# State-space layer on one Trainium2 core: two decoder products, their additions and the store of each batch put off into the next batch's turn

## What is computed

```
fx = _layernorm(u, ln1_g, ln1_b)
Bu = jnp.einsum('ph,blh->blp', B_bar, fx.astype(B_bar.dtype))
_, xs = jax.lax.associative_scan(binop, (lam_el, Bu), axis=1)
y = 2.0 * jnp.real(jnp.einsum('hp,blp->blh', Cc, xs)) + D * fx
y = jax.nn.gelu(y, approximate=False) + res
fy = _layernorm(y, ln2_g, ln2_b)
z = fy @ W_enc.T
z1, z2 = jnp.split(z, 2, axis=-1)
z = z1 * jax.nn.gelu(z2, approximate=False)
y = z @ W_dec.T + fy
```

## Time and profile before

| | us |
|---|---|
| median of 3 runs | 4407.61 |
| lowest and highest | 4402.94, 4409.49 |
| profiled execution, whole | 4405.0 |
| its span, first to last instruction | 4403.3 |
| of it the turns 0 to 7 of the state-space layer | 784.1 |

### The profile page before, as it was taken

The page is one execution under the profiler, slowest core; times in us unless marked ns, Lnnn a source line. Parts: engine busy times, 40 slices in busy tenths (PEclk is TensorE's granted clock), DMA queues, the critical chain, the costliest instruction groups (busy, mean ns, idle before and its releaser), DMA issues. The chain is left out here.

```text
span 4403.3 us, 53838 instructions
## 1 busy us (share of the span) xinstructions
PE 3966.2 (90%) x17283; PEld 2343.6 (53%) x17283; DVE 3071.4 (70%) x3124; ACT 2265.4 (51%) x3601; POOL 1375.6 (31%) x1108
## 2 busy tenths in 40 slices
PE   6999999999999999749999998455799999999999
PEld 5777777777777677414444443234344444444444
DVE  4757575767676766376777775434888879878878
ACT  2858686767676777533333322222445445544544
POOL 2758575757576767521111100213000000000000
PEclk8999999999999999969999999787899999999999
DMA  4323233333333333110111100647110110110110
GB/s 126 89 76 107 76 104 85 99 90 98 90 94 95 90 98 75 68 57 29 57 43 43 43 29 29 179 136 210 66 43 0 43 43 0 43 43 0 43 43 14
DMA packets 114250, 307.91 MB, mean 70 GB/s; under 512 B 47634, under 2 KB 49250, under 8 KB 104306
## 3 DMA queue, kind: packets, MB, share of 16 engines
q1 hardware_dynamic: 105522, 272.56, 20.1%
q0 software_dynamic: 7504, 24.80, 2.2%
q10 hardware_dynamic: 1008, 7.67, 0.5%
HBM read 203.12 MB, written 101.30 MB: 69 GB/s over the span
## 5 line engine op out<-in xcount | busy, mean ns | idle before, releaser
L417 POOL TENSOR_TENSOR probs_lo<-probs,probs_hi 128x512 fp32r<-128x512 f32 x848 | 1172.0, 1398 | 637.7 <-ACT probs L463 617.8
L530 DVE TENSOR_REDUCE maxima<-m_psum 128x1 fp32r<-128x1024 f32 x512 | 625.3, 1222 | 367.4 <-PE m_psum L706 366.6
L462 ACT ACTIVATE probs_hi<-s_psum 128x512 fp32r<-128x512 f32 x1024 | 614.0, 600 | 382.1 <-PE o_psum L735 220.4
L2376 PE MATMUL psum<-mixes,last_weights 128*128 128x512 f32 x1728 | 751.1, 592 | 0.0
L463 ACT ACTIVATE probs<-s_psum 128x512 f32<-128x512 f32 x1024 | 608.2, 594 | 0.0
L2376 PEld LDWEIGHTS psum<-mixes,last_weights 128*128 128x128 f32 x1728 | 327.5, 190 | 409.8 <-issue 409.8
L719 PE MATMUL s_psum<-q_all,k_hi 128*128 128x512 f32 x1024 | 429.7, 420 | 25.6 <-ACT probs L463 25.4
L735 PE MATMUL o_psum<-probs_lo,v 128*112 128x512 f32 x1024 | 411.9, 402 | 13.4 <-DVE probs_lo L610 6.6
L720 PE MATMUL s_psum<-q_all,k_lo 128*128 128x512 f32 x1024 | 403.6, 394 | 0.0
L730 PE MATMUL o_psum<-probs_hi,v 128*112 128x512 f32 x1024 | 403.3, 394 | 0.0
L2383 PE MATMUL psum<-xp,last_weights 128*128 128x512 f32 x864 | 382.2, 596 | 18.3 <-DVEq L2260 13.3
(11 more groups left out here) (327 smaller groups left out, 6025.4 us busy)
## 6 DMA issues: line engine op xcount, KB each, us to landing
xin<-x SPq DMA_DIRECT2D x17, 1536.0 KB, 6.9
xin<-in_x SPq DMA_DIRECT2D x16, 1536.0 KB, 7.5
k_hi<-k_rows_hi SPq DMA_DIRECT2D x128, 192.0 KB, 3.4
xres<-x SPq DMA_DIRECT2D x16, 1536.0 KB, 7.0
k_rows_hi<-stage_hi SPq DMA_DIRECT2D x48, 256.0 KB, 2.1
k_rows_lo<-stage_lo SPq DMA_DIRECT2D x48, 256.0 KB, 2.3
q_rows_hi<-stage_hi SPq DMA_DIRECT2D x48, 256.0 KB, 2.3
q_rows_lo<-stage_lo SPq DMA_DIRECT2D x48, 256.0 KB, 2.5
```

Source lines behind the costliest of these rows:

```text
L417: pool.tensor_tensor(probs_lo[:, u % RING, :], probs[:, u % RING, :], as_f32(probs_hi[:, u % RING, :]), ALU.subtract).then_inc(pool_low.ne ...
L462: nc.scalar.activation(probs_hi[:, u % RING, :], s_psum[:, u % 2, :], ACT.Exp, scale=SCALE)
L530: nc.vector.tensor_reduce(maxima[:, g % 2, tile:tile + 1], source, AX.X, ALU.max, negate=True).then_inc(rows_max.next(), 1)
L2376: ins = nc.tensor.matmul(bank, conv_w[:, t, down, factor, m * P:(m + 1) * P], mixes[:, factor, t, down:down + S, :].rearrange("p a b -> p ...
```

## The change

- A constant EARLY = 4. In turn i the decoder makes products 0 to 3 of batch i after its encoder; products 4 and 5 are made in turn i + 1, after the last norm sum and ahead of that turn's encoder. The last batch makes all six in its own turn. ORDER, and with it the banks, follows.
- VectorE's outputs is split alike: four additions and bn_stats in turn i; two more, with the moments, in turn i + 1 between the second half of turn_in (and the second norm's scaling) and the first norm's scaling.
- SyncE stores batch i - 1 and reloads xres for batch i in turn i, behind the load of xin.
- GpSimd's and ScalarE's sums and squares of the first norm use a tile of their own, first_sums, instead of hid.

```diff
+        first_sums = sb("first_sums", [P, CT, T])
...
+        EARLY = 4
+
+        def early(i):
+            return EARLY if i + 1 < B else 2 * CT
...
+            if i >= 1:
+                ORDER += [("dec", i - 1, n) for n in range(EARLY, 2 * CT)]
             if i >= 0:
-                ORDER += [("enc", i, n) for n in range(4 * CT)] + [("dec", i, n) for n in range(2 * CT)]
+                ORDER += [("enc", i, n) for n in range(4 * CT)] + [("dec", i, n) for n in range(early(i))]
...
-                if i >= 0:
-                    sp.wait_ge(out_made.sem, out_made.at(2 * CT, i))
-                    sp.dma_start(x_out[i:i + 1].rearrange("a (p t) n -> p (a t n)", t=CT), xres[:, :, :].rearrange("p t n -> p (t n)")).then_inc(stored, 16)
-                    if i + 1 < B:
-                        sp.wait_ge(out_measured.sem, out_measured.at(1, i))
-                        sp.wait_ge(stored, 16 * (i + 1))
...
+                if i >= 1:
+                    store(i - 1)
+                    sp.wait_ge(out_measured.sem, out_measured.at(1, i - 1))
+                    sp.wait_ge(stored, 16 * i)
...
+            store(B - 1)
...
-                        at = hid[:, 0, cols(half)]
+                        at = first_sums[:, 0, cols(half)]
...
-                    squares(norm1, hid, f1[i % 2], centred1, squared1, i + 2)
+                    squares(norm1, first_sums, f1[i % 2], centred1, squared1, i + 2)
...
-            def outputs(i):
-                for n in range(2 * CT + 1):
-                    if n < 2 * CT:
+            def outputs(i, first, end):
+                for n in range(first, end + 1):
+                    if n < end:
...
-                    if n > 0:
+                    if n > first:
...
+                if end < 2 * CT:
+                    return
...
+                if batch(i - 1):
+                    outputs(i - 1, EARLY, 2 * CT)
                 if third:
                     scale(norm1, f1[i % 2], inv_made1, scaled1, i + 2)
...
-                    outputs(i)
+                    outputs(i, 0, early(i))
...
-            def fill_dec(i):
-                for n in range(2 * CT):
+            def fill_dec(i, first, end):
+                for n in range(first, end):
                     m, half = n % CT, n // CT
-                    if m == 0:
+                    if m == 0 or n == first:
...
                 if here:
+                    if i >= 1:
+                        fill_dec(i - 1, EARLY, 2 * CT)
                     fill_enc(i)
-                    fill_dec(i)
+                    fill_dec(i, 0, early(i))
```

More of the change, by code:

```diff
@@ L1123, in _, with store @@
         def _(sp):
+            def store(i):
+                sp.wait_ge(out_made.sem, out_made.at(2 * CT, i))
+                sp.dma_start(x_out[i:i + 1].rearrange("a (p t) n -> p (a t n)", t=CT), xres[:, :, :].rearrange("p t n -> p (t n)")).then_inc(stored, 16)
             for i in range(-3, B):
@@ L1129, in _ @@
                     sp.dma_start(xin[:, :], x_in[i + 3:i + 4].rearrange("a (p t) n -> p (a t n)", t=CT)).then_inc(x_loaded, 16)
-                if i >= 0:
-                    sp.wait_ge(out_made.sem, out_made.at(2 * CT, i))
-                    sp.dma_start(x_out[i:i + 1].rearrange("a (p t) n -> p (a t n)", t=CT), xres[:, :, :].rearrange("p t n -> p (t n)")).then_inc(stored, 16)
-                    if i + 1 < B:
-                        sp.wait_ge(out_measured.sem, out_measured.at(1, i))
-                        sp.wait_ge(stored, 16 * (i + 1))
-                        sp.dma_start(xres[:, :, :].rearrange("p t n -> p (t n)"), x_in[i + 1:i + 2].rearrange("a (p t) n -> p (a t n)", t=CT)).then_inc(res_loaded, 16)
+                if i >= 1:
+                    store(i - 1)
+                    sp.wait_ge(out_measured.sem, out_measured.at(1, i - 1))
+                    sp.wait_ge(stored, 16 * i)
+                    sp.dma_start(xres[:, :, :].rearrange("p t n -> p (t n)"), x_in[i:i + 1].rearrange("a (p t) n -> p (a t n)", t=CT)).then_inc(res_loaded, 16)
+            store(B - 1)
             sp.wait_ge(stored, 16 * B)
@@ L1152, in _ @@
                     for half in range(2):
-                        at = hid[:, 0, cols(half)]
+                        at = first_sums[:, 0, cols(half)]
                         pool.wait_ge(squared1.sem, squared1.at(half + 1, i + 2))
-                        pool.tensor_tensor(at, at, hid[:, 1, cols(half)], ALU.add).then_inc(summed_sq1.next(), 1)
+                        pool.tensor_tensor(at, at, first_sums[:, 1, cols(half)], ALU.add).then_inc(summed_sq1.next(), 1)
                         pool.wait_ge(summed_sq1.sem, summed_sq1.at(2 * half + 1, i + 2))
-                        pool.tensor_tensor(at, at, hid[:, 2, cols(half)], ALU.add).then_inc(summed_sq1.next(), 1)
+                        pool.tensor_tensor(at, at, first_sums[:, 2, cols(half)], ALU.add).then_inc(summed_sq1.next(), 1)
         @block.scalar
@@ L1515, in _ @@
                 if third:
-                    sums(norm1, norm_psums[0], hid[:, 0, :], summed_x1, averaged1, i + 2)
+                    sums(norm1, norm_psums[0], first_sums[:, 0, :], summed_x1, averaged1, i + 2)
                 if after:
@@ L1523, in _ @@
                 if third:
-                    sums(norm1, norm_psums[0], hid[:, 0, :], summed_sq1, varied1, i + 2)
+                    sums(norm1, norm_psums[0], first_sums[:, 0, :], summed_sq1, varied1, i + 2)
                 if here:
+                    if i >= 1:
+                        fill_dec(i - 1, EARLY, 2 * CT)
                     fill_enc(i)
-                    fill_dec(i)
+                    fill_dec(i, 0, early(i))
                 if after:
```

## The result

| | before | after |
|---|---|---|
| median, us | 4407.68 (4402.94 to 4409.49, 4 runs) | 4383.95 (4380.87 to 4385.62, 4 runs) |
| ratio after / before | | 0.9947, 95% interval 0.9933 to 0.9961 |
| profiled execution, us | 4405.0 | 4384.55 |
| span, us | 4403.3 | 4382.8 |
| turns 0 to 7 of the state-space layer, us | 784.1 | 759.9 |

The change made the kernel 23.7 us faster; 22.2 were forecast. In the two profiled executions the layer gave 24.2 us. The program up to it was 2.1 us shorter and the rest behind it 5.9 us longer, 4.8 of them in the next layer (321.3 us before, 326.1 after, from its group matmul to that of the layer behind).

A forecast was written before the change was run, and what follows sets the result against it. TensorE bounds the layer; its idle time and half clock can be won. Covering them less new waits gives 26.6 us, less 4.4 for clock falls: net 22.2, so 4407.6 becomes 4385.4 us, range 4378 to 4396.

The forecast's parts named there:

- VectorE's wait for the second product: VectorE, ahead of the first norm's scaling: the second moved addition waits some 1.8 us for the second moved product.
- first gating ends: VectorE's first gating, queued behind scaling, moments and two scans, ends 50.32 us into the turn; it was over at 45.4.
- TensorE's new wait: Encoder's sixth block reuses the bank the first gating reads: TensorE waits 2.6 to 2.7 us in turns 1 to 4.
- turns 1 to 4 without the half clock: State-space layer with the clock at 1.00: these turns become 99.3 us each, 13.7 us won together.
- turn 6: It swaps 5.15 us of products for 5.15 and covers 0.3 us.
- turn 7: Two products fill 5.49 us of idle but begin under half clock: between 0.8 won and 1.0 lost, taken as 0.
- half clock behind the new waits: Clock falls behind two in three of the new waits in four turns, at 1.65 us each: 4.4 us lost.
- edits that were costed at nothing: Own tile for the first norm's sums, and SyncE's later store and reload of xres: no cost, 15 us of cover.
- (a): Rival: the clock never falls about the new wait; 26.6 us won, 4381.0 us; chance 0.22.
- (b): Rival: moved products run at half clock for 3.4 us; 13.7 us won, 4393.9 us; chance 0.06.
- (c): Rival: moved products at half clock throughout, VectorE stands for them; slower, median 4416 us; chance 0.04.
- (d): Rival: gap stays as a moved product or xres reload is late; within 4 us of before; 0.05 with the like.

The follow-up runs named there:

- affine-first run: Kernel before, nothing put off, ScalarE making the second norm's affine step of the first half ahead of the first norm's logarithms: median 4386.39 against 4407.38 us, ratio 0.9955.

## Why the prediction was right

Step by step, turn 2 (and the others where named):

| step | forecast | measured |
|---|---|---|
| moved products start, us into the turn | 29.71 | 2228.57 - 2198.77 = 29.80 |
| encoder starts | 34.86 | 34.95 |
| VectorE's wait for the second product | 1.8 | 1.82 |
| scaling of f starts | 37.66 | 37.74 |
| first gating ends | 50.32 | 50.40 |
| TensorE's new wait | 2.6 to 2.7 | 2.47 of idle, 2.63 between matmul starts |
| turns 1 to 4 without the half clock | 99.3 | 99.5 |
| turn 0, turn 5 | 98.7, 96.7 | 98.71, 96.77 |
| turn 6 | 0.3 won | 91.82 to 91.21, 0.6 won |
| turn 7 | 0 | 73.28 to 72.02, 1.3 won |
| half clock behind the new waits | 4.4 us | turns 1 and 2: 1.5 + 1.7 = 3.2 us |

The 2.63 us are 2249.23 less the start of the encoder (2233.72) and five products of 2.575 us. The sum of the measured gains is 5.15 in turn 0, 410.99 - 401.19 = 9.8 in turns 1 to 4, 7.4 in turn 5, 0.6 and 1.3: 24.2 us. The forecast sum was 22.2. The two terms that were mis-sized by more than 1 us are both clock. Two of four falls came, not 2.7; the price of one was right (1.5 to 1.7 against 1.65). Two smaller ones are not: a turn without the half clock was 0.2 us longer than the forecast's 99.3, 0.8 in four turns, and turn 6 gave 0.3 more. And in turn 7 the moved products were taken to lose 1.7 to 3.4 us to the half clock; they lost 0.5, since it was back at 1.00 by 2701, 0.9 us after their start. The norm sums ahead of them had run for 3.8 us without a break:

```profile
2696.43 3.78 PE L831 MATMUL norm<-z,col_mean 128*128 128x512 f32 x4 [3.17 <-DVE z L1374]
2700.00 5.75 PE L1501 MATMUL psum<-hid,dec_w 128*128 128x512 f32 x12
2705.70 31.17 PE L1490 MATMUL psum<-y,enc_w 128*128 128x512 f32 x72
```

and the clock over the first 0.8 us of the products and the rest of them:

```profile
2700.00:2700.80 0.80, 0.80 (x2) 0.50 0.00 0
2701.00:2705.70 4.70, 4.70 (x12) 1.00 0.00 0
```

How near the sum came is in part luck. The number of falls was a guess, and a layer that stood 0.9 us later in time had one of them and not two. The medians differ by 23.7 us, while the two profiled executions differ by 20.5, since the rest of the program moved by a few microseconds too. What was understood, and not lucky, is the chain: the gap filled, VectorE's wait of 1.8 us, the late gating, and TensorE's new wait, each within 0.2 us.

The edits that were costed at nothing cost nothing. The store is issued 35.9 us into turn 2 and the reload 41.0 (forecast: 36 and back by 48), and add_residual (L1348) at 2262.15, 63.4 us in, follows the gating before it without a wait. SyncE's rows, the DMA-issuing instructions:

```profile
2234.70 0.33 SPq L1135 DMA_DIRECT2D x<-xres  x1
2239.76 0.33 SPq L1147 DMA_DIRECT2D xres<-x  x1
```

The rivals: (a), no half clock at all, would have been 26.6; turns 3 and 4 went that way. (b) and (c), the moved products at half clock, did not occur in any of turns 1 to 5. The reason given against (b), that a 1.63 us gap alone leaves the clock at 1.00, was weaker than it looked: in the affine-first run one such gap was followed by the half clock. (d) fell with the first rows. The Trainium skill's section on PSUM bank cycling ("TensorE: Matmul & The Clock Gate", "A second HAM failure mode: psum-queue depth-cycling") says that cycling through PSUM banks idles the array between groups of matmuls often enough for its clock to swing between the two levels. It named the right danger. The trace agrees in part: the wait on a bank of the ring, once a turn, was followed by the half clock in two of four turns, at 1.5 to 1.7 us each.

## What to carry to other kernels

An idle stretch of TensorE may cost more than its length: here some 2 us of half clock came on top of 4.1 us of idle, and useless work in the gap won 10 us in the whole kernel. When work is put into a gap of one engine, count what its consumers must do on the next engine and when: the order on VectorE, not the amount moved, decided whether the two products gave 24 or 37 us. When a product is put off, its addition comes late too, and whatever stands behind that addition on its engine pays; so put the addition where the product is surely done, and statistics behind whatever frees a bank.

## What the runs showed of the hardware

- Whether a wait of 2.3 to 2.5 us was followed by the half clock depended on where it lay in time, and this repeated: two profiles of one kernel had it in the same turns, and a shift of 0.9 or 1.6 us moved it to the turns named in advance. I had expected other turns in the second profile.
- In all profiles together, 10 of 21 such waits were followed by the half clock. Each fall began between 0.4 us before the wait's end and 1.5 us after it, lasted 3.4 us and cost 1.7 us, or 1.5 where its first 0.3 to 0.4 us still lay in the wait; one that fell ahead of a wait for another engine cost nothing, as the wait shrank by it.
- Where no gap of 4.08 us stood behind it, a gap of 1.6 us in turns 0 to 5 left the clock at 1.00 every time but one (turn 1 of the affine-first run). What exactly is wanted of TensorE was not measured.
